# Splitting attention weights in a pair's first half, and moving the output's transposes behind the row maxima

## The reference, cut to what matters

```python
probs = softmax(xf @ Wg.T + bg)                      # gates over 8 experts, the top 2 kept in combine
h = einsum('td,erd->ter', xf, A) + ba                # low-rank part, 8 experts x rank 16
delta = (einsum('ter,eor->to', h * combine, Bm) + combine @ bb) * 2
qkv = xf @ Wqkv.T + bqkv + delta                     # 1250 x 2304, 12 heads of 64
attn = softmax(q @ k.T * 64 ** -0.5)
out = (attn @ v) @ Wproj.T + bproj
```

## Time and profile before

| | us |
|---|---|
| three timed runs | 2957.41, 2965.63, 2967.86 (median 2965.63) |
| profiled execution, its own time | 2959.68 |
| its span | 2957.9 |
| PE busy in the span | 2637.5 (89%) |
| DVE busy | 1599.5 (54%) |
| POOL busy | 1266.3 (43%) |
| ACT busy | 778.0 (26%) |

### The profile page before, as it was taken

The page is one execution under the profiler, slowest core; times in us unless marked ns, Lnnn a source line. Parts: engine busy times, 40 slices in busy tenths (PEclk is TensorE's granted clock), DMA queues, the critical chain, the costliest instruction groups (busy, mean ns, idle before and its releaser), DMA issues.

```text
span 2957.9 us, 68470 instructions
## 1 busy us (share of the span) xinstructions
PE 2637.5 (89%) x24343; PEld 2008.1 (68%) x24343; DVE 1599.5 (54%) x3130; ACT 778.0 (26%) x1111; POOL 1266.3 (43%) x1376
## 2 busy tenths in 40 slices
PE   5998999978998859999999788986959999999989
PEld 4787888847676647888885667664537666666665
DVE  6576666654446654333333345546776646646631
ACT  2111121201222212211130121320135355365350
POOL 1685211147777745300005677773005164264271
PEclk9999999999999969999999899997979899999999
DMA  5233333459888966433236988998110000000013
GB/s 165 91 126 103 120 123 121 132 200 313 309 299 311 312 201 193 156 121 104 94 99 211 320 283 306 320 314 280 42 38 2 22 22 1 22 22 1 22 49 94
DMA packets 103837, 448.79 MB, mean 152 GB/s; under 512 B 20725, under 2 KB 21048, under 8 KB 99381
## 3 DMA queue, kind: packets, MB, share of 16 engines
q0 software_dynamic: 60352, 283.01, 28.5%
q1 hardware_dynamic: 40661, 123.20, 13.1%
q10 hardware_dynamic: 2592, 39.32, 3.9%
HBM read 361.50 MB, written 83.92 MB: 151 GB/s over the span
## 4 chain that ended last, share of the span: by engine, by line
PE 58%; DVE 17%; issue 8%; POOL 5%; DVEq 5%; DMA 4%; ACT 2%; POOLq 0%; ACTq 0%; SPq 0%
PE PS L1796 26%; PE PS L1806 4%; PE PS L2091 3%; PE PS L2174 3%; PE PS L1895 2%; PE PS L2157 2%; PE PS L1998 2%; DVE NMC L1716 2%; PE PS L1927 2%; PE PS L2158 2%; POOL GATA L732 2%; DVE RCP L1441 2%; POOL PL L769 2%; POOL ROW L732 1%; DMA MSG<-msg_table,SKEY 1%
## 5 line engine op out<-in xcount | busy, mean ns | idle before, releaser
L1796 PE MATMUL PS<-WHL,XT 128*125 (+1 forms) x2880 | 488.7, 329 | 6.3 <-DVE WHL L1132 4.2
L1796 PE MATMUL PS<-WHL,HT 128*125 (+1 forms) x2880 | 476.8, 328 | 13.2 <-DVE HT L1285 10.7
L1796 PEld LDWEIGHTS PS<-WHL,HT 128*125 (+1 forms) x2880 | 394.7, 138 | 91.6 <-DVE HT L1285 12.5
L1796 PEld LDWEIGHTS PS<-WHL,XT 128*125 (+1 forms) x2880 | 391.7, 138 | 82.6 <-issue 4.7
L769 POOL TENSOR_TENSOR PL<-PF 125x500 bf16<-125x500 f32 (+1 forms) x306 | 291.9, 981 | 252.6 <-ACT PF L984 248.8
L732 POOL DMA_INDIRECT GATA<-msg_table,SKEY x324 | 312.4, 964 | 144.0 <-issue 90.6
L1219 DVE SCALAR_TENSOR_TENSOR MSG<-PS,MSG 125x768 f16<-125x768 f32 x160 | 153.1, 957 | 353.0 <-ACT MSG L808 351.1
L808 ACT ACTIVATE MSG<-PS 125x768 f16<-125x768 f32 x160 | 129.6, 810 | 795.8 <-PE PS L1796 785.4
L732 POOL DMA_INDIRECT ROW<-msg_table,SKEY x216 | 213.7, 990 | 92.8 <-issue 60.5
L984 ACT ACTIVATE PF<-PS,QK 125x500 f32<-125x500 f32 (+1 forms) x360 | 212.8, 608 | 103.0 <-PE PS L2158 102.8
L2174 PE MATMUL PS<-V,PF 125*125 125x129 bf16 x1200 | 194.6, 258 | 26.3 <-POOL PL L769 24.2
(11 more groups left out here) (327 smaller groups left out, 4905.5 us busy)
## 6 DMA issues: line engine op xcount, KB each, us to landing
msg_table<-MSG SPq DMA_DIRECT2D x160, 336.0 KB
WST<-in_wg_dram ACTq DMA_DIRECT2D x16, 2304.0 KB, 10.3
WST<-in_wf_dram SPq DMA_DIRECT2D x7, 1536.0 KB, 6.2
KROW<-key_rows POOLq DMA_DIRECT2D x54, 192.0 KB, 3.8
WST<-in_wm_dram SPq DMA_DIRECT2D x6, 1152.0 KB
msg_table<-MSG SPq DMA_DIRECT2D x160, 39.0 KB
GATA<-msg_table,SKEY POOLq DMA_INDIRECT x324
ROW<-msg_table,SKEY POOLq DMA_INDIRECT x216
```

What stands on the lines that cost most here:

```text
L1796: ins = pe.matmul(PS[0:ROWS, b0 + h, 0:HALF], X[:, xp, k, bass.ts(t, ROWS)], panel_part(slot, wp, k, h), start=k == 0 and xp + wp == 0, st ...
```

## The change

The next pair's weights are split in the first half of a pair. GpSimd makes the scales directly behind `panel_top`. ScalarE writes the high parts ahead of `q1` in `HIGHS`. A new function on GpSimd, `panel_low`, makes the low parts: it multiplies the staged float32 values by their scales in place and subtracts the high parts. VectorE's `split_low` leaves the loop. `FH` and `FL` get two slots that are used by parity, at the cost of 384 float32 of `FILL`, an unused tensor. The scale of the products (`XWINV`), which the running pair still needs, is made apart at tile 34. `ON_DVE` has eleven tiles where it had nine. The transposes `X0` to `X2` move from behind `q0` to behind `R`, into banks 1, 0 and 3, and ScalarE copies them out behind `NMT` where it did so ahead of `k0`.

```diff
@@ -138,10 +138,10 @@
         WPR = sb(pctx, "WPR", [128, KT * D], f32)
         pctx.close()
         qctx = top.enter_context(ExitStack())
-        FH = sb(qctx, "FH", [128, 2, 3 * 128], f16)
+        FH = sb(qctx, "FH", [128, 2, 2, 3 * 128], f16)
         FL = sb(qctx, "FL", [128, 2, 3 * 128], f16)
         QS = sb(qctx, "QS", [128, 2, N], f16)
-        FILL = sb(qctx, "FILL", [128, KT * D - 6 * 128 - N], f32)
+        FILL = sb(qctx, "FILL", [128, KT * D - 9 * 128 - N], f32)
         ROWS4 = sb(top, "ROW", [128, 4, D], f32)
         ROW = ROWS4[0:ROWS]
         GATR = ROWS4[:].bitcast(f16)
@@ -327,8 +327,6 @@
                     FFN.append((f"v{t // 4}", "dve", ((4, 5, 2)[t // 4],)))
 
         part("q0", 0, KT + 1)
-        for c in range(3):
-            FFN.append((f"X{c}", "act", ((0, 1, 3)[c],)))
         part("k0", 0, KT + 1)
         part("k1", 0, 4)
         for n_, (x, first, end) in enumerate((("k1", 4, 5), ("k1", 5, 6), ("k1", 6, 7), ("k2", 0, 3))):
@@ -345,11 +343,13 @@
             values(1 if n_ < 20 or n_ in (21, 23, 24, 25, 26, 27, 29) else 0)
         values(1)
         FFN.append(("R", "act", (0,)))
+        for c in range(3):
+            FFN.append((f"X{c}", "act", ((1, 0, 3)[c],)))
         values(2 * RT)
         HIGHS = ("q0", "k0", "k1", "k2", "q1", "q2", "v0", "v1", "v2")
         LOWS = ["q0", "k0"] + TOPS[0:12] + ["k1", "k2"] + TOPS[12:30] + ["v0", "v1", "v2", "q1", "q2"] + [f"O{h}{c}" for h in range(2) for c in range(3)]
-        SPLIT_AT = 38
-        ON_DVE = (7, 11, 17, 21, 27, 31, 37, 41, 57)
+        NEXT_SCALE = 34
+        ON_DVE = (7, 11, 17, 20, 22, 31, 37, 41, 47, 50, 52)
 
 
         LAG = 4
@@ -735,7 +735,6 @@
             def ffn_scales():
 
                 g.tensor_scalar(SCI[:, WSCALE], SCI[:, POW], -1.0, float((254 + TOP) << 23), ALU.mult, ALU.add)
-                g.tensor_scalar(SC[:, XWINV], SC[:, POW], RS[:, UP], 2.0 ** -TOP / X_SCALE, ALU.mult, ALU.mult)
                 g.drain()
                 g.tensor_tensor(RS[:, FSC], SC[:, WSCALE], RS[:, RANKS], ALU.mult)
                 g.drain()
@@ -743,10 +742,34 @@
                 g.drain()
                 g.sem_inc(S["w_scale"], 1)
 
+            def product_scale():
+
+                g.tensor_scalar(SC[:, XWINV], SC[:, POW], RS[:, UP], 2.0 ** -TOP / X_SCALE, ALU.mult, ALU.mult)
+                g.drain()
+
+            def panel_low(q):
+
+                g.wait_ge(S["w_hi"], q + 1)
+                g.sem_inc(S["tick"], 1)
+                slot = bass.ds(q % 2, 1)
+                g.tensor_scalar(WST[:, WM:WM + 3 * 128], WST[:, WM:WM + 3 * 128], RS[:, FSC], None, ALU.mult)
+                g.tensor_scalar(WST[:, 0:WM], WST[:, 0:WM], SC[:, WSCALE], None, ALU.mult)
+                g.drain()
+                g.tensor_scalar(WST[32:64, WM + 3 * 128:WF], WST[32:64, WM + 3 * 128:WF], RS[32:64, FSC], None, ALU.mult)
+                g.drain()
+                high = FH[:, slot].rearrange("p a k c -> p (a k c)")
+                g.tensor_tensor(FL[:, slot].rearrange("p a c -> p (a c)"), WST[:, WM:WM + 3 * 128], high[:, 0:3 * 128], ALU.subtract)
+                g.tensor_tensor(WHM[:, slot, 1, :].rearrange("p a c -> p (a c)"), WST[:, 0:WM], WHM[:, slot, 0, :].rearrange("p a c -> p (a c)"), ALU.subtract)
+                g.drain()
+                g.tensor_tensor(high[32:64, 3 * 128:6 * 128], WST[32:64, WM + 3 * 128:WF], high[32:64, 3 * 128:6 * 128], ALU.subtract)
+                g.drain()
+                g.sem_inc(S["w_lo"], 1)
+
             panel_top(W_FFN)
             g.wait_ge(S["lg_free"], RT + 2)
             g.wait_ge(S["rank_scale"], 1)
             g.sem_inc(S["tick"], 1)
+            product_scale()
             ffn_scales()
             g.drain()
             g.memset(KX[DH:DH + 1, :, :], SHIFT)
@@ -757,11 +780,13 @@
             g.sem_inc(S["ffn_ready"], 1)
             with g.Fori(0, PAIRS) as it:
                 panel_top(it + (W_FFN + 1))
+                ffn_scales()
+                panel_low(it + (W_FFN + 1))
                 for n_ in range(2 * 3 * RT):
                     h, c, t = n_ // 30, n_ // 10 % 3, n_ % 10
                     n = CHUNKS[c][1]
-                    if n_ == SPLIT_AT - 4:
-                        ffn_scales()
+                    if n_ == NEXT_SCALE:
+                        product_scale()
                     if n_ in ON_DVE:
                         continue
                     g.wait_ge(S["ffn_act"], ffn.taken(it, f"S{h}{c}{t}"))
@@ -789,7 +814,7 @@
             def split_ranks(q):
 
                 act.wait_ge(S["w_scale"], q + 1)
-                act.activation(FH[:].rearrange("p k c -> p (k c)"), WST[:, WM:WF], ACT.Copy, scale=RS[:, FSC])
+                act.activation(FH[:, bass.ds(q % 2, 1)].rearrange("p a k c -> p (a k c)"), WST[:, WM:WF], ACT.Copy, scale=RS[:, FSC])
                 split_high(q, W=WHM, cols=WM)
 
             def load_panel(q):
@@ -960,13 +985,14 @@
                     act.activation(HF[:, bass.ds(to, 1), c0:c0 + n].rearrange("p a c -> p (a c)"), PS[:, ffn.bank(f"X{c}"), 0:n], ACT.Copy).then_inc(S["ffn_act"], 1)
 
                 for r in HIGHS:
-                    if r == "k0":
-                        for c in range(3):
-                            output_columns(c, (it + PAIRS - 1) % PAIRS)
+                    if r == "q1":
+                        split_ranks(it + (W_FFN + 1))
                     if r == "v2":
                         act.wait_ge(S["ffn_pe"], ffn.made(it, "R"))
                         act.wait_ge(S["row_in"], it * 16 + 16)
                         act.activation(NMT[:], PS[0:2 * RT, ffn.bank("R"), 0:ROWS], ACT.Copy, scale=1.0 / SHIFT).then_inc(S["ffn_act"], 1)
+                        for c in range(3):
+                            output_columns(c, (it + PAIRS - 1) % PAIRS)
                     if r[0] == "v":
                         v_high(int(r[1]))
                     else:
@@ -976,8 +1002,6 @@
                     h, c, t = n_ // 30, n_ // 10 % 3, n_ % 10
                     n = CHUNKS[c][1]
                     p = PS[0:ROWS, ffn.bank(f"S{h}{c}{t}"), 0:n]
-                    if n_ == SPLIT_AT:
-                        split_ranks(it + (W_FFN + 1))
                     act.wait_ge(S["ffn_pe"], ffn.made(it, f"S{h}{c}{t}"))
 
                     act.wait_ge(S["av_done"], it * 60 + (n_ + 1))
@@ -1028,8 +1052,8 @@
 
                 v.wait_ge(S["w_hi"], q + 1)
                 if ranks:
-                    v.scalar_tensor_tensor(FL[:, 0, :], WST[:, WM:WM + 3 * 128], RS[:, FSC], FH[:, 0, :], ALU.mult, ALU.subtract)
-                    v.scalar_tensor_tensor(FH[32:64, 1, :], WST[32:64, WM + 3 * 128:WF], RS[32:64, FSC], FH[32:64, 1, :], ALU.mult, ALU.subtract)
+                    v.scalar_tensor_tensor(FL[:, q % 2, :], WST[:, WM:WM + 3 * 128], RS[:, FSC], FH[:, q % 2, 0, :], ALU.mult, ALU.subtract)
+                    v.scalar_tensor_tensor(FH[32:64, q % 2, 1, :], WST[32:64, WM + 3 * 128:WF], RS[32:64, FSC], FH[32:64, q % 2, 1, :], ALU.mult, ALU.subtract)
                 v.scalar_tensor_tensor(W[:, bass.ds(q % 2, 1), 1, 0:cols].rearrange("p a c -> p (a c)"), WST[:, 0:cols], SC[:, WSCALE],
                                        W[:, bass.ds(q % 2, 1), 0, 0:cols].rearrange("p a c -> p (a c)"), ALU.mult, ALU.subtract).then_inc(S["w_lo"], 1)
 
@@ -1719,8 +1743,6 @@
                         normalise(ffn.bank(r), n, c0, h)
                         v.sem_inc(S["ffn_dve"], 1)
                         v.drain()
-                        if r == "O10":
-                            split_low(it + (W_FFN + 1), WHM, WM, ranks=True)
 
             with v.Fori(0, RT // 2) as i:
                 for j in range(2):
@@ -2076,7 +2098,7 @@
                 def ranks(x):
 
                     c = slice(x * 128, (x + 1) * 128)
-                    return ((FH[:, 0, c], LTH[:, 0, :]), (FH[:, 0, c], LTL[:]), (FL[:, 0, c], LTH[:, 0, :]), (FH[0:96, 1, c], LTH[0:96, 1, :]))
+                    return ((FH[:, slot, 0, c], LTH[:, 0, :]), (FH[:, slot, 0, c], LTL[:]), (FL[:, slot, c], LTH[:, 0, :]), (FH[0:96, slot, 1, c], LTH[0:96, 1, :]))
 
                 def keys_or_queries(nm, c, first, end):
 
@@ -2181,10 +2203,10 @@
 
             pe.wait_ge(S["ffn_dve"], ffn.taken(PAIRS - 1, "O12"))
             for c in range(3):
-                ffn.wait_banks(pe, PAIRS, f"X{c}")
+                pe.wait_ge(S["ffn_act"], ffn.taken(PAIRS - 1, "S129"))
                 output_transposes(c)
             pe.wait_ge(S["wp_in"], 32)
-            pe.wait_ge(S["ffn_act"], ffn.taken(PAIRS, "X2"))
+            pe.wait_ge(S["ffn_act"], ffn.taken(PAIRS - 1, "S129") + 3)
             for i in range(RT // 2):
                 for j in range(2):
                     pe.wait_ge(S["fp_free"], i * 2 + (j + 1))
```

## The result

The changed kernel takes 2926.18 us (median of 4 runs, 2923.80 to 2933.71), the kernel before 2961.52 us (4 runs, 2956.89 to 2967.86). The ratio is 0.9874, 95% interval 0.9852 to 0.9896: faster by 1.26%, 35.3 us at the medians, where 24 were forecast. Before's median stands 4 us under the one that the prediction was made with.

The account below looks back on a forecast made before the run. TensorE's largest wait was for GpSimd's low parts, 24.2 us in 35 gaps. Per pair 6.0 + 0.6 + 0.3 - 3.7 = 3.2 us, six times 19.2, plus 5.0 for five heads, 24 in all: 2938 us, range 2914 to 2957.

Parts of the forecast that it names:

- `score_scale`: First half: VectorE's two-input column operation waits 2.7 us for GpSimd's scaling; with 1.0 for the clock, 3.7 lost a pair.
- clock at the heads: Start of the next pair: less time at half clock, 1.0 us gained at each of five heads, bounds -1.0 to 2.4.
- transposes: Moved from behind `q0` to behind `R`, partly under the row's DMA: 0.3 us gained a pair, between 0 and 1.07.
- VectorE's split: Its leaving the second half makes the last narrow stretch run like the earlier one: 6.0 us gained a pair.
- ScalarE's split: Its leaving the second half speeds tiles 30 to 49: 0.6 us gained a pair, bounds 0 to 1.4.
- Delays nothing: SP's next load, which waits for `w_lo`, stands behind the row's DMA in SP's order and was said to delay nothing.
- The cover: First half: ScalarE's split fits its idle time ahead of `q1`; GpSimd's work ends 12 us before its first `PL`.
- No wait at all: Rival: at `score_scale` the column operations slip between GpSimd's or do not conflict; 2916 us, chance 0.22.
- A long wait: Rival: VectorE waits 5.5 us at `score_scale`, 1.7 more for the clock; 2960 us, no measurable change, chance 0.13.
- GpSimd late: Rival: in the second half's narrow stretches `PL` still comes too late, 6.0 shrinks to 3; 2956 us, chance 0.09.
- VectorE held through all of `panel_low`: Rival: VectorE gets the port only after all of `panel_low`, waiting 11.9 us a pair; 3008 us, slower, chance 0.06.

Follow-up runs that it names:

- split alone: The changed kernel with the transposes and their copies put back behind `q0`: 2932.21 us against 2964.89 for the kernel before, ratio 0.9894.
- idle operations: The changed kernel with nine VectorE tiles, plus three unread operations at the old split's place: 2980.69 us with two SBUF inputs, 2931.48 with one.
- nine tiles on VectorE: The changed kernel with the `ON_DVE` list of the kernel before: 2915.13 us in one run, against 2966.16 for the kernel before.
- The filled pause: The changed kernel with five unread matmuls between a pair and the next: 2921.07 us against 2966.16 for the kernel before, ratio 0.9855.

## Why the prediction was right in kind and 12 us short

The forecast was 24 us gained out of the sum, 2938. Measured are 34.7 in the profiles and 35.3 at the medians. By the prediction's own terms, in us over the six pairs:

| term | forecast | measured | how |
|---|---|---|---|
| second half: VectorE's and ScalarE's split leave | +39.6 | +44.1 | first to last exp, six pairs |
| `score_scale`, with the clock | -22.2 | -11.4 | 5 x 0.96, and 6.5 in pair 0 |
| clock at the heads | +5.0 | +2.3 | five heads, split alone, less the wait |
| transposes | +1.8 | -0.3 | heads +4.9, row to first exp -5.2 |
| sum | +24.2 | +34.7 | |

**VectorE's split** was forecast at 6.0 a pair and is worth 6.24 to 6.83, 6.4 on average. The prediction read both narrow stretches some 0.2 us too long, since tile 50 starts at 2405.15 and nine narrow tiles take 5.28 and not 5.5; the difference of the two is as it said. That the cause is two engines that exclude each other was read off durations; the idle operations at the same place show it, and cost 38.5 of the 44.1 us again. That the number of SBUF inputs decides is what these two runs and the undelayed L1695 say together. The Trainium skill (SBUF — State Buffer, "SBUF: two separate sides") has the lock between a VectorE operation with two SBUF inputs and a GpSimd operation that reads SBUF, and the runs agree: 3.33 us against 1.46 for the longest `PL`.

**ScalarE's split** was worth 0.92 a pair, 0.6 forecast, inside its bounds: tiles 30 to 49 went from 18.27 to 17.35 us (17.17 with nine tiles on VectorE).

**`score_scale`** is the term that was most mis-sized: 22.2 us of loss were forecast and 11.4 measured, where the whole sum is 10.5 short. The mechanism and the moment were right: it comes 4.74 us behind the scaling's start in pair 1, 4.7 forecast. The scaling was priced at 7.4 us, from 324 elements in 1.21; 2304 take 6.11, 2.65 ns an element and not 3.1, and the waiting operation is through 0.44 ahead of the recorded end. What is left of 2.7 us is 0.77 in the record and 0.96 at `NMT`, and the clock did not fall behind it. So the 1.0 for the clock was wrong in five pairs as well. In pair 0, which the prediction didn't read by itself, the scaling begins 1.30 us ahead of `score_scale`; the wait is 4.2, the clock falls, and the pair loses 6.5 (from `score_scale` to `NMT` 25.93 us, 19.38 before). The Trainium skill (GPSIMD Engine Reference, "Elementwise — side-by-side cycle accounting") has 769 ns for 512 elements of a tight loop, from which the estimate for the scaling was 3.5 us. The trace says 6.11, so the two prices were wrong on opposite sides, the row's by 21% and the estimate from the page by 43%.

**The heads**: the 14 us at half clock behind the split are gone, yet in four of five heads the clock falls behind the normalisation's pause, for 3.4 us where the end of the last pair suggested 6.8. So a head gained 0.46 us by the clock, 1.0 forecast, and `q0` takes 5.66 us, just over the 5.5 that was given as its upper end. The filled pause shows that the fall needs this pause; that it came in 22 of 30 unfilled heads says that the pause alone doesn't decide it.

**The transposes** did nothing of use inside the layer. The forecast of 0.3 a pair had both sides of it right in kind, a head gains 0.98 and the row's wait hides the rest only in part (0.5 us lost). Not foreseen were 0.8 and 1.2 us in pairs 3 and 5, where the row's DMA takes 3.50 and 3.86. "Delays nothing" was right for the load of the weights. What stretches the row is open. It comes only with the transposes behind `R`: with them behind `q0` the row took 2.06 to 2.20 us in these two pairs, in three kernels. One packet of the queue that the profile calls "instruction" lies beside the row then, but such packets lie beside it in pair 1 too, and in the kernel before, without a delay. No run tells them apart.

**The cover** held: ScalarE's split fitted into its idle time, and `panel_low` ran from 25.9 to 41.6 us behind the start of pair 1, ending 14 us ahead of the first exp (2356.97, 2371.17).

**The rivals.** No wait at all fell (the wait is there in every pair), though the total came close to the middle between it and the forecast. A long wait holds for pair 0 alone. GpSimd late fell: 5.28 us, as in the earlier narrow stretch. VectorE held through all of `panel_low` fell: it waited for the end of one operation.

## What to carry to other kernels

Before work is laid beside another engine's, look at what each of the two reads: an operation on one column can wait for all of a long one on the other engine, and a small one can often be moved to a place where that engine is idle. Check the first turn of a loop by itself, since its events can lie otherwise than in the turn that was read, and the one bad turn cost more here than the five others together. When TensorE stalls, count the slow clock behind it as well; a short filling of the pause costs nothing if TensorE would wait there anyway.

## What the runs showed of the hardware

- VectorE's operation on two SBUF columns, held up by one of GpSimd's, ended 0.44 us ahead of that one's recorded end, in pairs 0 and 1 alike. The profile counts the wait as its duration, 0.93 and 4.37 us, and not as idle time.
- Four VectorE operations with one input in PSUM and one in SBUF took 2.49 us beside GpSimd's scaling, as long as without it.
- GpSimd's `tensor_scalar` with a column as factor took 1.26 us for 384 elements and 6.11 for 2304, which is 2.53 ns an element and 0.29 us fixed; the row of 1.21 us for 324 that the price was taken from the earlier trace rows lies above that line. A subtraction with a float16 input took 0.91 for 384 and 4.56 for 2304 (5.1 forecast). On 32 partitions it costs what it costs on 128: 0.90.
- An idle time of TensorE of 1.2 us at the head, with smaller gaps ahead of it, was followed by a fall of the clock in four of five heads. Five matmuls in it kept the clock up in all 15 heads of three kernels.
- A DMA of 4.9 KB took 2.06 to 2.20 us in most pairs. In all nine kernels with the transposes behind `R` it took 3.08 to 3.86 in two of six, always the same two, in the run that held the load of weights back as well.
